# A graph network on one core: node groups moved behind an edge pass, and row weighting moved from VectorE to ScalarE

## The chip, the core and the metric

The kernel runs on one core of one Trainium2 chip. The metric is the device time of one execution in microseconds. The engines have short names in the profile: PE is TensorE (matmuls), PEld its weight loads, DVE is VectorE, ACT is ScalarE, POOL is GpSimd (here it only issues indirect DMAs, which fetch or scatter rows by an index table) and SP is SyncE (it issues plain DMAs). Each engine works through its own list of instructions in order and waits on semaphores that the others raise.

## The reference

A graph with 100,000 nodes of 128 features and 50,000 edges, sorted by destination, goes through four residual layers, each followed by a layer norm (`_layernorm`):

```python
x = _layernorm(x + L0(x))   # three sparse products Z = A Z; concat[x, Z1, Z2, Z3] @ W + b
x = _layernorm(x + L1(x))   # MLP (128 -> 256 -> 128) of x and sum, max, mean of edge attributes
x = _layernorm(x + L2(x))   # attention over the edges: q, k, v, skip; softmax by destination
x = _layernorm(x + L3(x))   # (x + 3 A x) / 4
```

A sparse product A Z fetches row `src` of Z for each edge, multiplies it by the edge's weight, and sums the rows of edges with the same destination:

```python
msgs = edge_vals[:, None] * Z[edge_col]
return jax.ops.segment_sum(msgs, edge_row, num_segments=N_NODES)
```

Only destinations of edges have anything but zero in A x. All other nodes depend on their own row alone.

## The kernel before

Rows are handled in groups of 512 (four tiles of 128). There are 196 node groups, in 49 iterations of four (the four buffer slots), and 98 edge groups, in 25 iterations. The kernel does all nodes as if they had no edges, does the rows that edges touch besides, and scatters the corrected rows over the result at the end. In order of time:

1. Preparation, with a sort of the indices on VectorE, while GpSimd fetches the rows of the destinations.
2. The node stage: `N0` = 11 iterations of node groups alone. A node group is `chain_a` (first product), a norm, `chain_b1` (turn), `chain_b2` (first MLP layer), `chain_c` (second MLP layer, L1125), a norm, `chain_d1` and `chain_d2` (turn, skip product), a norm.
3. The first pass: 25 iterations with a node group and an edge group in each step. The edge group's rows are fetched by GpSimd (`z_gather(0)`), weighted, turned so that edges lie along the free axis, scanned with `tensor_tensor_scan` (a running sum per destination), turned back and stored.
4. The second pass: `N2` = 13 iterations with a node group and two edge groups in each step (`z_gather(1)`). It needs the stored sums of the whole first pass.
5. The source stage: for each edge group the third product (`z_gather(2)`, `z_weigh(2)`, `z_turn(2)`, `z_scan(2)`) and the fetch of the source's own row (`x_gather`, `x_turn`, `x_src`), then the first two layers for these rows; beside it scans over the edge attributes (`attr_scan`).
6. The destination stage, the attention stage, and the last stage: `z_gather(3)`, `z_weigh(3)`, turn, `z_scan(3)`, turn back, `fin_sum`, square, `power` (row sums of squares), `std`, and the final norm, which GpSimd scatters into the output. In the last stage 13 of 25 iterations of results are held in free buffers until the plain copy of the node results, 28 pieces issued by ScalarE (`copy_pieces`), has ended.

In between GpSimd issues small index scatters (`codes`, L788), 392 in all; the counts `VB0`, `VB1`, `VC0`, `VG1` to `VG3` say how many stand where. `VB1` stand ahead of the first pass, `VC0` are spread over its groups, `VG1` stand behind it.

The order of each engine is written out with `steps`. Each stage of a list has a lag: at step g the engine does that stage for group g minus lag, in the order of the list. In the source stage the lists, with lags, are, on TensorE: turn of x1 (2), `chain_a` (1), `chain_b2` (2), turn of x2 (4), `z_turn` (0), `x_turn` (0), `chain_c` (3), skip (4); on VectorE:

```python
steps(dve, EI, (norm2("s"), 4), (z_weigh(2), 0), (power("s", 0), 1), (norm1("s"), 1), (z_scan(2), 0),
      (layer2("s"), 3), (power("s", 1), 3), (attr_scan, 0), (power("s", 2), 4), (attr_mean, 0),
      (norm("s", 2, lambda s: bSK, x3, "ln3_out", x3_free), 4), peeled=1)
```

on ScalarE:

```python
steps(act, EI, (square("s", 0), 1), (std("s", 0), 1), (relu("s"), 2), (seed_mm1("s"), 0), (x2_out("s"), 4),
      (x_src, 0), (square("s", 1), 3), (seed_mlp("s"), 2), (std("s", 1), 3), (x1_out("s"), 1), (square("s", 2), 4),
      (std("s", 2), 4), peeled=1)
```

So at step g VectorE weighs group g, sums the rows of g - 1, scans g, and does layer2 of g - 3. `std` waits for `power` of the same group, `z_turn` for `z_weigh`, `z_scan` for `z_turn`, `layer2` for `chain_c`. A fetch into a slot waits for the turn of the group that was in the slot before. Many operations share a line: L1008 are all turns on TensorE, L1958 all row sums, L1973 all norms, L1989 all weightings, L2008 all scans, L751 all fetches, L764 all scatters of rows. The tiles tell them apart: `gat` holds the fetched rows.

Of the kernel before, what the change touches and what calls it, by code (L numbers as in the profile page):

```python
# [26 lines left out]
P = 128  # L27
T = 4
# [15 lines left out]
def gnn_kernel(nc, x_fm, x_rows, src_g, dst_g, dnext_g, src_flat, dst_flat, w_flat, attr_fm,  # L44
# [14 lines left out]
    N2 = -(-EI // 2)  # L59
    N0 = NI - EI - N2  # L60
    LF = P
# [13 lines left out]
    with ctx:  # L75
# [3 lines left out]
        def dram(name, shape, dt=F32):  # L79
# [12 lines left out]
            "q_out": ("x1T", NI + 2 * EI), "decay": ("relu", NI + 2 * EI), "weight": ("x2T", NI + EI),  # L92
            "att_src": ("z_rows", 2 * EI), "gathered_x": ("gathered_d", 0), "ld_attr": ("st_xd", EI * 16),
        }
# [243 lines left out]
        PAYC = 32  # L338
        VB0, VB1, VC0, VG1, VG2, VG3 = 34, 60, 98, 40, 36, 24
        assert XD0 % SL == 0 and EG - XD0 <= (N0 - 1) * SL and PAYC <= N0 * SL and LF % PAYC == 0  # L340
        assert VB0 + VB1 + VC0 + VG1 + VG2 + VG3 <= EC and LF * 4 <= SL * G
# [13 lines left out]
        def half(stage, e):  # L355

            def one(i, s):
                zi = i * 2 + s // 2
                if not isinstance(i, int) or zi < EI:
                    stage(zi, (2 * s + e) % SL)  # L360
            return one

# [49 lines left out]
        def seq(k, i):  # L412
            return i + k * EI
# [25 lines left out]
        def _(sp):  # L439
# [150 lines left out]
            def pay_store(i, s):  # L590
                k = i * SL + s
                if k < PAYC:
# [7 lines left out]

            steps(sp, EI, (node_load(N0), 0), (x1_store(N0), 3), (zT_store(0), 4), (zE_store(0), 6), (x4_store(N0), 5),
                  (spmm_rows(0), 1), peeled=1)

            steps(sp, N2, (node_load(N0 + EI), 0), (x1_store(N0 + EI), 3), (two(zT_store(1)), 4), (x4_store(N0 + EI), 5),
                  (two(spmm_rows(1)), 2), (two(zE_store(1)), 5), peeled=1)
# [320 lines left out]
        def _(pe):  # L926
# [203 lines left out]
            def chain_d1(kind, i, s):  # L1130
# [5 lines left out]
                if kind == "d":  # L1136
                    prior(pe, "x2sel", s, i)
                else:

                    ahead = (s + 2) // SL  # L1140
                    ends_at = {"node": [N0, N0 + EI, NI], "s": [EI]}[kind]
# [40 lines left out]
            b1, a, b2, d1, c, d2 = node(N0)  # L1182
            steps(pe, EI, b1, a, (z_turn(0), 2), b2, d1, c, (z_back(0), 3), d2, peeled=1)
            all_slots(pe, "x2T", N0 + EI)
            b1, a, b2, d1, c, d2 = node(N0 + EI)
            steps(pe, N2, b1, a, (half(z_turn(1), 0), 2), (half(z_back(1), 0), 3), b2, d1, c, (half(z_turn(1), 1), 2),
# [81 lines left out]
        def _(act):  # L1268
# [139 lines left out]
            def codes_out(i, s):  # L1408
                if void(act, i, s, ("codes_out", i, 1)):
# [6 lines left out]
            steps(act, N0, *node(0))  # L1416
            steps(act, EI, *node(N0)[:6], (z_rows(0), 4), (codes_out, 2), *node(N0)[6:], peeled=1)
            steps(act, N2, *node(N0 + EI)[:6], (half(z_rows(1), 1), 4), *node(N0 + EI)[6:9],
                  (half(z_rows(1), 0), 3), *node(N0 + EI)[9:], peeled=1)
            all_slots(act, "st_z2", 2 * EI * 16)  # L1420

            def x_src(i, s):
                if void(act, i, s, ("x_src", i, 1)):
# [4 lines left out]

            steps(act, EI, (square("s", 0), 1), (std("s", 0), 1), (relu("s"), 2), (seed_mm1("s"), 0), (x2_out("s"), 4),
                  (x_src, 0), (square("s", 1), 3), (seed_mlp("s"), 2), (std("s", 1), 3), (x1_out("s"), 1), (square("s", 2), 4),  # L1430
# [45 lines left out]

            steps(act, EI, (copy_pieces, 0), (square("fin", 3), 2), (std("fin", 3), 2), unrolled=True)


        @block.vector  # L1480
        def _(dve):
# [578 lines left out]
            p0, n1, l2, p1, p2, n2, n3 = node(N0)  # L2060
            steps(dve, EI, p0, (z_scan(0), 2), n1, l2, (z_weigh(0), 1), p1, p2, n2, n3, peeled=1)
            all_slots(dve, "codes_out", EI)
            p0, n1, l2, p1, p2, n2, n3 = node(N0 + EI)
            steps(dve, N2, p0, (half(z_scan(1), 0), 2), n1, l2, (half(z_weigh(1), 0), 1), p1, p2,
# [22 lines left out]
            def attr_mean(i, s):  # L2087
                if void(dve, i, s, ("attr_mean", i, 1)):
# [4 lines left out]

            steps(dve, EI, (norm2("s"), 4), (z_weigh(2), 0), (power("s", 0), 1), (norm1("s"), 1), (z_scan(2), 0),
                  (layer2("s"), 3), (power("s", 1), 3), (attr_scan, 0), (power("s", 2), 4), (attr_mean, 0),
# [147 lines left out]

            def fin_free(i, s):
                if i == HB - 2:
                    at(dve, "st_x3_", s, 2 * EI * 16)
                elif i == HB:
                    at(dve, "scattered2", s, moved(1, 0, s))
                elif i > HB:
                    reuse(dve, "scattered", s, i - HB, 64)  # L2250

            def fin_norm(i, s):
                dst = [h.rearrange("p (t f) -> p t f", t=T) for h in held[i]] if i < HB else x4s
                norm("fin", 3, lambda s: t2[s], dst, "ln4_out", fin_free)(i, s)

            steps(dve, EI, (z_weigh(3), 0), (power("fin", 3), 3), (z_scan(3), 1), (fin_norm, 3), (fin_sum, 2), unrolled=True)


# [51 lines left out]
```

## Time and profile before

| what | value |
|---|---|
| median of 3 runs | 6072.8 us (6069.09 to 6074.92) |
| the profiled execution | 6074.08 us, its span 6072.2 us |
| busy: PE, PEld | 4362.9 us (72%), 3182.1 us (52%) |
| busy: DVE, ACT, POOL | 4394.4 us (72%), 3146.3 us (52%), 4430.8 us (73%) |
| TensorE's mean granted clock | 0.869 of full speed |
| data moved | 1151.65 MB |

Shares of the whole span say little here, since the stages have different limits; the prediction reads each stage by itself. In a timeline a row is one instruction or several alike that follow each other (x4). The bracket tells how long the engine stood idle before it, and what released it; "issue" is time in which nothing that the profile shows was waited for.

### The profile page before, as it was taken

Reading aid. Unit: us, or ns where it says so; the run is one execution under the profiler, and the core shown is the slowest. Engines: PE = TensorE matmul, PEld = TensorE weight load, DVE = VectorE, ACT = ScalarE, POOL = GpSimd, SP = SyncE. Lnnn points to the kernel's source line nnn. Section 1 sums busy time; section 2 is a strip of 40 time slices with the busy share of each in tenths; the row PEclk is TensorE's granted clock in tenths of the full one; section 3 lists DMA queues with packets and bytes.
Section 4 is the critical chain, followed back from the end, with each engine's and each line's share of the span. In section 5 each row is a group of like instructions: output and inputs, shape, how many; then the busy total and the mean of one; then the engine's idle time right before and its main releaser. Section 6 shows DMA issues by size and latency. Waiting matters only on the chain. (4 is left out here: it accounts for less than half of the span.)

```text
span 6072.2 us, 102714 instructions
## 1 busy us (share of the span) xinstructions
PE 4362.9 (72%) x25328; PEld 3182.1 (52%) x25328; DVE 4394.4 (72%) x8168; ACT 3146.3 (52%) x6667; POOL 4430.8 (73%) x4339
## 2 busy tenths in 40 slices
PE   1059899998888799999989999888878873422200
PEld 0047688886666677777765555544444442211100
DVE  8966699997888688888865555599999995743300
ACT  0047688886666455555544444378888881110000
POOL 7777566667777777777757777577777766777777
PEclk9999999999999899999999999988888885555555
DMA  5377488886888799999977777634444438943311
GB/s 126 100 142 181 132 250 253 251 250 197 286 285 286 198 262 264 263 262 264 262 199 224 226 225 227 197 106 116 114 117 114 114 104 265 328 133 94 92 40 40
DMA packets 1005231, 1151.65 MB, mean 190 GB/s; under 512 B 184599, under 2 KB 641235, under 8 KB 1004182
## 3 DMA queue, kind: packets, MB, share of 16 engines
q1 hardware_dynamic: 831958, 834.69, 46.0%
q0 software_dynamic: 137984, 247.24, 16.8%
q10 hardware_dynamic: 35136, 68.16, 3.1%
q14 instruction: 115, 0.94, 0.1%
q8 instruction: 38, 0.62, 0.0%
HBM read 688.22 MB, written 523.68 MB: 200 GB/s over the span
## 5 line engine op out<-in xcount | busy, mean ns | idle before, releaser
L1008 PE MATMUL bank<-ident,gat 128*128 128x128 f32 x2352 | 423.6, 309 | 633.2 <-DVE zT L2008 558.9
L1111 PE MATMUL bank<-x1T,W1x 128*128 128x512 f32 x1568 | 764.9, 600 | 24.5 <-ACT x1T L1304 24.5
L1125 PE MATMUL bank<-W2s,hT 128*128 128x128 f32 x6272 | 777.8, 277 | 1.0 <-ACT hT L1388 1.0
L1125 PEld LDWEIGHTS bank<-W2s,hT 128*128 128x128 f32 x6272 | 734.5, 193 | 16.8 <-ACT hT L1388 1.7
L1008 PEld LDWEIGHTS bank<-ident,gat 128*128 128x128 f32 x2352 | 305.0, 161 | 760.1 <-issue 576.2
L1314 ACT ACTIVATE mbuf<-t 128x512 f32<-128x512 f32 x490 | 309.9, 633 | 581.3 <-DVE t L2042 309.3
L1388 ACT ACTIVATE hT<-bank,b1u 128x512 f32<-128x512 f32 x784 | 502.9, 679 | 183.7 <-PE bank L1111 183.4
L751 POOL DMA_INDIRECT gat<-XD,s_q x392 | 376.8, 961 | 243.1 <-ACT codes_z L1414 109.8
L1008 PE MATMUL bank<-ident,x 128*128 128x128 f32 x3136 | 481.7, 277 | 94.6 <-DVE x L1973 84.6
L751 POOL DMA_INDIRECT gat<-X,d_x x392 | 397.4, 1014 | 205.3 <-issue 205.0
L788 POOL DMA_INDIRECT VQ<-s_v,s_q x392 | 448.7, 1145 | 119.5 <-issue 117.6
L764 POOL DMA_INDIRECT Y<-x,d_out x392 | 403.4, 1029 | 173.2 <-issue 110.9
L1008 PEld LDWEIGHTS bank<-ident,x 128*128 128x128 f32 x3136 | 371.0, 142 | 283.8 <-DVE x L1973 169.3
L751 POOL DMA_INDIRECT gat<-X,s_src x392 | 402.2, 1026 | 153.4 <-issue 153.1
L1989 DVE TENSOR_TENSOR gat<-gat,wts 128x512 f32<-128x512 f32 x294 | 202.8, 690 | 424.8 <-DMA gat<-X,codes_z 372.4
L751 POOL DMA_INDIRECT gat<-Z2E,codes_z x392 | 419.5, 1070 | 119.9 <-issue 119.6
L751 POOL DMA_INDIRECT x<-in_x_rows,s_src x392 | 414.6, 1058 | 119.5 <-issue 119.5
L2008 DVE TENSOR_TENSOR_SCAN zT<-fB,zT,bank 128x512 f32<-128x512 f32 x392 | 498.1, 1271 | 2.4 <-PE bank L1008 2.2
L751 POOL DMA_INDIRECT zin_<-in_x_rows,mixa x392 | 399.6, 1019 | 130.1 <-issue 112.9
L751 POOL DMA_INDIRECT gat<-X,codes_z x392 | 382.3, 975 | 130.1 <-issue 119.0
L751 POOL DMA_INDIRECT gat<-Z1E,codes_z x392 | 379.3, 968 | 119.5 <-issue 104.2
L1111 PEld LDWEIGHTS bank<-x1T,W1x 128*128 128x128 f32 x1568 | 277.5, 192 | 270.9 <-issue 244.5
(369 smaller groups left out, 11316.5 us busy)
## 6 DMA issues: line engine op xcount, KB each, us to landing
X<-x SPq DMA_DIRECT2D x588, 256.0 KB, 2.6
fB<-row_s_same SPq DMA_DIRECT2D x392, 256.0 KB, 5.1
Y<-x SPq DMA_DIRECT2D x294, 256.0 KB, 3.7
xT<-in_x_fm SPq DMA_DIRECT2D x196, 256.0 KB
ffB<-rows_last_notlast SPq DMA_DIRECT2D x98, 512.0 KB
out_rows<-Y ACTq DMA_DIRECT2D x28, 1792.0 KB
Z1T<-zT SPq DMA_DIRECT2D x98, 256.0 KB
Z1E<-zE SPq DMA_DIRECT2D x98, 256.0 KB
```

The lines of the kernel that those rows point to most:

```text
L751: pool.indirect_dma_start(out=tile[:, t, 0:width], out_offset=None, in_=table, in_offset=bass.IndirectOffsetOnAxis(ap=index[t], axis=0)).t ...
L764: pool.indirect_dma_start(out=table, out_offset=bass.IndirectOffsetOnAxis(ap=index[t], axis=0), in_=rows[t], in_offset=None, bounds_check= ...
L788: pool.indirect_dma_start(out=VQ, out_offset=bass.IndirectOffsetOnAxis(ap=s_q[:, c:c + 1], axis=0), in_=s_v[:, c:c + 1], in_offset=None, b ...
L1008: mm = pe.transpose(dst[:, t, :], tiles[t], ident[:, :])
L1111: mm = pe.matmul(bH[h][:, :, :], W1x[:, cols], x1T[s][:, :], start=kind != "d", stop=True)
L1125: mm = pe.matmul(bMLP[:, t, :], hT[h][s][:, t * P:(t + 1) * P], W2s[:, h, :], start=False, stop=h == HC - 1, skip_group_check=True)
L1314: act.activation(sq[k % 3][s % 2], [bT1, t2[s], bSK, t2[s]][k][:, :, :], ACT.Square).then_inc(S(f"squared{k}", s), 1)
L1388: a = act.activation(hT[h][s][:, :], flat(bH[h]), ACT.Relu, bias=b1u[:, h:h + 1])
L1989: dve.tensor_tensor(gat[s][:, :, 0:P], gat[s][:, :, 0:P], weight.to_broadcast([P, T, P]), ALU.mult).then_inc(S("weighted", s), 1)
L2008: dve.tensor_tensor_scan(zT[s][:, :], fB[s][:, :], flat(bIN), zT[s - 1][:, G - 1:G], ALU.mult, ALU.add).then_inc(S("scanned", s), 1)
```

## The change

First, `N1 = EI + 2`: the loop of the first pass becomes 27 iterations, in whose last two only node groups are done, and `N0` falls from 11 to 9. The edge stages in that loop are wrapped in `passing`, which leaves them out from iteration 25 on. 34 index scatters move from ahead of the first pass (`VB1` 60 to 26) into it (`VC0` 98 to 132). Second, the weighting of the source stage and of the last stage goes from VectorE (one `tensor_tensor` of 128x512) to ScalarE (four `activation` with Copy, 128x128 each, the weight as a scale per partition). Third, the last norm's multiplication goes to ScalarE in the same form (`fin_norm`), while VectorE keeps the reciprocal (`fin_scale`). The diff, without the lines that only follow from the new count:

```diff
-    N0 = NI - EI - N2
+    N1 = EI + 2
+    N0 = NI - N1 - N2
...
-        VB0, VB1, VC0, VG1, VG2, VG3 = 34, 60, 98, 40, 36, 24
+        VB0, VB1, VC0, VG1, VG2, VG3 = 34, 26, 132, 40, 36, 24
...
+        def passing(stage):
+
+            def one(i, s):
+                if not isinstance(i, int) or i < EI:
+                    stage(i, s)
+            return one
...
-            steps(pe, EI, b1, a, (z_turn(0), 2), b2, d1, c, (z_back(0), 3), d2, peeled=1)
+            steps(pe, N1, b1, a, (passing(z_turn(0)), 2), b2, d1, c, (passing(z_back(0)), 3), d2, peeled=N1 - EI + 1)
...
+            def z_weigh(k):
+
+                def stage(i, s):
+                    c = seq(k, i)
+                    if void(act, i, s, ("weighted", c, 1)):
+                        return
+                    at(act, "gathered", s, moved(5 if k == 3 else k, i + 1, s))
+                    for t in range(T):
+                        w = bass.ds((i * SL + s) * T + t, 1)
+                        a = act.activation(gat[s][:, t, 0:P], gat[s][:, t, 0:P], ACT.Copy, scale=wts[:, w])
+                    a.then_inc(S("weighted", s), 1)
+                return stage
...
-            steps(act, EI, (square("s", 0), 1), (std("s", 0), 1), (relu("s"), 2), (seed_mm1("s"), 0), (x2_out("s"), 4),
+            steps(act, EI, (square("s", 0), 1), (std("s", 0), 1), (relu("s"), 2), (z_weigh(2), 0), (seed_mm1("s"), 0),
+                  (x2_out("s"), 4),
...
-            steps(act, EI, (copy_pieces, 0), (square("fin", 3), 2), (std("fin", 3), 2), unrolled=True)
...
+            def fin_norm(i, s):
+                if void(act, i, s, ("ln4_out", x4i("fin", i), 1)):
+                    return
+                ready(act, "scaled", s, i)
+                fin_free(i, s)
+                dst = held[i][s].rearrange("p (t f) -> p t f", t=T) if i < HB else x4[s]
+                for t in range(T):
+                    a = act.activation(dst[:, t, :], t2[s][:, t, :], ACT.Copy, scale=lns[3][2][s][:, t:t + 1])
+                a.then_inc(S("ln4_out", s), 1)
+
+            all_slots(act, "agg_turned", EI)
+            steps(act, EI, (copy_pieces, 0), (z_weigh(3), 0), (fin_norm, 3), (square("fin", 3), 2), (std("fin", 3), 2),
+                  unrolled=True)
...
-            steps(dve, EI, (norm2("s"), 4), (z_weigh(2), 0), (power("s", 0), 1), (norm1("s"), 1), (z_scan(2), 0),
+            steps(dve, EI, (norm2("s"), 4), (power("s", 0), 1), (norm1("s"), 1), (z_scan(2), 0),
...
+            def fin_scale(i, s):
+                if void(dve, i, s, ("scaled", i, 1)):
+                    return
+                _, sd, rs, _ = lns[3]
+                ready(dve, "deviation3", s, i)
+                at(dve, "ln4_out", s, x4i("fin", i))
+                dve.reciprocal(rs[s][:, :], sd[s][:, :]).then_inc(S("scaled", s), 1)
+
+            steps(dve, EI, (power("fin", 3), 3), (z_scan(3), 1), (fin_scale, 3), (fin_sum, 2), unrolled=True)
```

## Rows read from the trace of the kernel before

**Rows 1.** Table of two stages (source, attention): busy time, granted clock, DMA.

```profile
2011.00:3145.00 1134.00, 1018.81 (x7411) 853.21 (x7412) 960.32 (x1460) 604.92 (x1265) 860.46 (x808) 0.99 0.92 253
3936.00:5034.00 1098.00, 862.04 (x3234) 499.55 (x3234) 1003.10 (x2454) 902.77 (x1858) 805.36 (x784) 0.81 0.40 112
```

**Rows 2.** Timeline of GpSimd: start, duration, line, tiles; in brackets idle before and releaser.

```profile
723.95 0.96 POOL L751 DMA_INDIRECT gat<-XD,s_q  x1 [34.80 <-PE bank L1008]
...
1406.41 0.97 POOL L751 DMA_INDIRECT gat<-XD,s_q  x1 [1.28 <-ACT codes_z L1414]
...
1465.12 0.99 POOL L751 DMA_INDIRECT gat<-Z1E,codes_z  x1 [0.30 <-issue]
...
1485.79 0.94 POOL L751 DMA_INDIRECT gat<-Z1E,codes_z  x1 [0.30 <-issue]
...
2009.69 0.98 POOL L788 DMA_INDIRECT VQ<-s_v,s_q  x1 [0.31 <-issue]
2010.98 0.99 POOL L751 DMA_INDIRECT gat<-Z2E,codes_z  x1 [0.30 <-issue]
...
3083.15 0.94 POOL L751 DMA_INDIRECT x<-in_x_rows,s_src  x1 [0.30 <-issue]
...
3145.11 0.98 POOL L751 DMA_INDIRECT gat<-X,d_x  x1 [27.29 <-issue]
```

**Rows 3.** Timeline of VectorE in the source stage.

```profile
2019.87 0.69 DVE L1989 TENSOR_TENSOR gat<-gat,wts 128x512 f32<-128x512 f32 x1 [9.57 <-DMA gat<-Z2E,codes_z]
...
3104.98 0.68 DVE L1958 TENSOR_REDUCE ln1vr<-mbuf 128x4 f32<-128x512 f32 x1
...
3108.14 0.66 DVE L2042 SCALAR_TENSOR_TENSOR t<-x,bank 128x512 f32<-128x512 f32 x1
3109.50 0.69 DVE L1958 TENSOR_REDUCE ln2vr<-mbuf 128x4 f32<-128x512 f32 x1 [0.70 <-ACT mbuf L1314]
...
3115.59 0.68 DVE L1989 TENSOR_TENSOR gat<-gat,wts 128x512 f32<-128x512 f32 x1
3116.19 0.68 DVE L1958 TENSOR_REDUCE ln1vr<-mbuf 128x4 f32<-128x512 f32 x1
```

**Rows 4.** Timeline of TensorE, first turn of the second pass.

```profile
1479.24 0.60 PE L1008 MATMUL bank<-ident,gat 128*128 128x128 f32 x4
```

**Rows 5.** Groups of instructions by form, ScalarE: busy us, mean ns.

```profile
L1353 ACT ACTIVATE x<-t,ln3nm,ln3rs 128x128 f32<-128x128 f32 x392 | 160.0, 479 | 1.9 <-DVE ln4nm L2207 1.9
...
L1340 ACT ACTIVATE ln4sd<-lmv,mixb,mixa 128x1 f32<-128x1 f32 x392 | 118.1, 372 | 0.0
...
L1328 ACT ACTIVATE ln2sd<-ln2vr,epsc 128x4 f32<-128x4 f32 x392 | 116.3, 297 | 70.4 <-DVE ln2vr L1958 70.3
```

**Rows 6.** Timeline of ScalarE in the same source round.

```profile
3105.69 0.30 ACT L1328 ACTIVATE ln1sd<-ln1vr,epsc 128x4 f32<-128x4 f32 x1 [2.60 <-DVE ln1vr L1958]
3105.90 1.25 ACT L1388 ACTIVATE hT<-bank,b1u 128x512 f32<-128x512 f32 x2
3107.07 0.59 ACT L1293 COPY bank<-seed_a 128x512 f32<-128x512 f32 x1
```

**Rows 7.** Timeline of TensorE in the same source round.

```profile
3104.51 0.65 PE L1008 MATMUL bank<-ident,x 128*128 128x128 f32 x4 [0.44 <-DVE x L1973]
3105.12 0.66 PE L1008 MATMUL bank<-ident,gat 128*128 128x128 f32 x4
...
3106.05 1.95 PE L1125 MATMUL bank<-W2s,hT 128*128 128x128 f32 x16
```

**Rows 8.** Timeline of TensorE as the source stage drains.

```profile
3144.42 1.12 PE L1008 MATMUL bank<-ident,x 128*128 128x128 f32 x4 [4.65 <-DVE x L1973]
3145.33 3.36 PE L1125 MATMUL bank<-W2s,hT 128*128 128x128 f32 x16
```

**Rows 9.** Timeline of VectorE in the last stage, a round without waits.

```profile
5074.93 0.68 DVE L1989 TENSOR_TENSOR gat<-gat,wts 128x512 f32<-128x512 f32 x1
...
5078.94 0.68 DVE L1989 TENSOR_TENSOR gat<-gat,wts 128x512 f32<-128x512 f32 x1
```

More of the change, by code:

```diff
@@ L92, in gnn_kernel @@
             "q_out": ("x1T", NI + 2 * EI), "decay": ("relu", NI + 2 * EI), "weight": ("x2T", NI + EI),
-            "att_src": ("z_rows", 2 * EI), "gathered_x": ("gathered_d", 0), "ld_attr": ("st_xd", EI * 16),
+            "att_src": ("z_rows", 2 * EI), "scaled": ("scale34", EI), "gathered_x": ("gathered_d", 0), "ld_attr": ("st_xd", EI * 16),
         }
@@ L338, in gnn_kernel @@
         PAYC = 32
-        VB0, VB1, VC0, VG1, VG2, VG3 = 34, 60, 98, 40, 36, 24
-        assert XD0 % SL == 0 and EG - XD0 <= (N0 - 1) * SL and PAYC <= N0 * SL and LF % PAYC == 0
+        VB0, VB1, VC0, VG1, VG2, VG3 = 34, 26, 132, 40, 36, 24
+        assert XD0 % SL == 0 and EG - XD0 <= N0 * SL and PAYC <= N0 * SL and LF % PAYC == 0
         assert VB0 + VB1 + VC0 + VG1 + VG2 + VG3 <= EC and LF * 4 <= SL * G
@@ L599, in _ @@
                   unrolled=True)
-            steps(sp, EI, (node_load(N0), 0), (x1_store(N0), 3), (zT_store(0), 4), (zE_store(0), 6), (x4_store(N0), 5),
-                  (spmm_rows(0), 1), peeled=1)
-            steps(sp, N2, (node_load(N0 + EI), 0), (x1_store(N0 + EI), 3), (two(zT_store(1)), 4), (x4_store(N0 + EI), 5),
+            steps(sp, N1, (node_load(N0), 0), (x1_store(N0), 3), (passing(zT_store(0)), 4), (passing(zE_store(0)), 6),
+                  (x4_store(N0), 5), (passing(spmm_rows(0)), 1), peeled=N1 - EI + 1)
+            steps(sp, N2, (node_load(N0 + N1), 0), (x1_store(N0 + N1), 3), (two(zT_store(1)), 4), (x4_store(N0 + N1), 5),
                   (two(spmm_rows(1)), 2), (two(zE_store(1)), 5), peeled=1)
@@ L1140, in chain_d1 @@
                     ahead = (s + 2) // SL
-                    ends_at = {"node": [N0, N0 + EI, NI], "s": [EI]}[kind]
+                    ends_at = {"node": [N0, N0 + N1, NI], "s": [EI]}[kind]
                     end = next((e for e in ends_at if i < e), 0) if isinstance(i, int) else 0
@@ L1182, in _ @@
             b1, a, b2, d1, c, d2 = node(N0)
-            steps(pe, EI, b1, a, (z_turn(0), 2), b2, d1, c, (z_back(0), 3), d2, peeled=1)
-            all_slots(pe, "x2T", N0 + EI)
-            b1, a, b2, d1, c, d2 = node(N0 + EI)
+            steps(pe, N1, b1, a, (passing(z_turn(0)), 2), b2, d1, c, (passing(z_back(0)), 3), d2, peeled=N1 - EI + 1)
+            all_slots(pe, "x2T", N0 + N1)
+            b1, a, b2, d1, c, d2 = node(N0 + N1)
             steps(pe, N2, b1, a, (half(z_turn(1), 0), 2), (half(z_back(1), 0), 3), b2, d1, c, (half(z_turn(1), 1), 2),
@@ L1416, in _ @@
             steps(act, N0, *node(0))
-            steps(act, EI, *node(N0)[:6], (z_rows(0), 4), (codes_out, 2), *node(N0)[6:], peeled=1)
-            steps(act, N2, *node(N0 + EI)[:6], (half(z_rows(1), 1), 4), *node(N0 + EI)[6:9],
-                  (half(z_rows(1), 0), 3), *node(N0 + EI)[9:], peeled=1)
+            steps(act, N1, *node(N0)[:6], (passing(z_rows(0)), 4), (passing(codes_out), 2), *node(N0)[6:],
+                  peeled=N1 - EI + 1)
+            steps(act, N2, *node(N0 + N1)[:6], (half(z_rows(1), 1), 4), *node(N0 + N1)[6:9],
+                  (half(z_rows(1), 0), 3), *node(N0 + N1)[9:], peeled=1)
             all_slots(act, "st_z2", 2 * EI * 16)
+            def z_weigh(k):
[9 more added lines that the diff above has]
+                return stage
             def x_src(i, s):
@@ L1475, in copy_pieces, with fin_free @@
                     act.dma_start(out_runs[w, :], src_runs[w, :]).then_inc(S("copied"), 16)
-            steps(act, EI, (copy_pieces, 0), (square("fin", 3), 2), (std("fin", 3), 2), unrolled=True)
+            def fin_free(i, s):
+                if i == HB - 2:
+                    at(act, "st_x3_", s, 2 * EI * 16)
+                elif i == HB:
+                    at(act, "scattered2", s, moved(1, 0, s))
+                elif i > HB:
+                    reuse(act, "scattered", s, i - HB, 64)
+            def fin_norm(i, s):
[10 more added lines that the diff above has]
+                  unrolled=True)
         @block.vector
@@ L2060, in _ @@
             p0, n1, l2, p1, p2, n2, n3 = node(N0)
-            steps(dve, EI, p0, (z_scan(0), 2), n1, l2, (z_weigh(0), 1), p1, p2, n2, n3, peeled=1)
+            steps(dve, N1, p0, (passing(z_scan(0)), 2), n1, l2, (passing(z_weigh(0)), 1), p1, p2, n2, n3,
+                  peeled=N1 - EI + 1)
             all_slots(dve, "codes_out", EI)
-            p0, n1, l2, p1, p2, n2, n3 = node(N0 + EI)
+            p0, n1, l2, p1, p2, n2, n3 = node(N0 + N1)
             steps(dve, N2, p0, (half(z_scan(1), 0), 2), n1, l2, (half(z_weigh(1), 0), 1), p1, p2,
@@ L2242, in fin_sum @@
                                          op0=ALU.mult, op1=ALU.add).then_inc(S("fin_sum", s), 1)
[L2244 to L2256, printed above, removed]
+            def fin_scale(i, s):
[6 more added lines that the diff above has]
+            steps(dve, EI, (power("fin", 3), 3), (z_scan(3), 1), (fin_scale, 3), (fin_sum, 2), unrolled=True)
 def kernel(**inputs):
```

## The prediction

> **What bounds the kernel now.** I read the page first, then one table by stage, then the timeline of each engine inside the stages that the change touches. The page's chain of what ended last is of little use here, since it covers only the last tenth and shows GpSimd. The table by stage says more [rows 1]: in the source stage VectorE is busy 960.32 of 1134 us and ScalarE 604.92, so ScalarE looks like the place with room.
>
> GpSimd's timeline shows where each stage begins [rows 2]. It waits 34.80 us for the end of the node stage before group 4 of the first pass; in that pass it waits about 1.28 us a group, at a pace of 7.34 us (723.95 to 1406.41 is 93 groups). It fetches without a gap from 1465.12 to 2010.98, and in the source stage from there to 3083.15, so 1072 us for 98 groups or 10.94 us each. Then it waits 27.29 us until 3145.11. So the source stage does not end with its fetches.
>
> VectorE's timeline of that stage shows the reason [rows 3]. One round (one edge group) lasts 11.21 us, from the first norm's row sums at 3104.98 to the next at 3116.19. The last weighting is at 3115.59, some 30 us after the last fetch. VectorE works through its round with only short waits, so the round is a loop through VectorE's own order, and 97 of them last from 2019.87 to 3115.59.
>
> **The change, part by part. Eight node groups** go from the node stage to behind the first pass. The work is the same and the order within a group is too, so I cost the move itself at nothing: 144 node groups, with their loads and stores on SyncE's queue, stand ahead of the second pass either way. What moves is GpSimd. The first pass begins eight groups of some 7.3 us earlier, so its last fetch does, and the 40 index scatters behind it end near 1407 instead of 1465. The first 16 fetches of the second pass then lie in their four buffers before anyone wants them. The 17th needs the first turn of the second pass, which TensorE does at 1479.24, 0.60 long [rows 4], behind node work that stays where it was. So the 17th fetch starts near 1480.0 instead of 1485.79 [rows 2]: 5.8 us gained, kept to the end of the second pass because GpSimd has no gap from there on. The 34 scatters moved into the first pass cost 1.29 us each (2009.69 to 2010.98) [rows 2]: 34 × 1.29 = 44 us against 93 × 1.28 = 119 us of waits, so nothing. Without that cover they would cost 44 us. Where they came from, they stood before the 34.80 us wait.
>
> **Weighting in the source stage.** VectorE loses one instruction of 0.60 us a round (3115.59 to 3116.19) [rows 3]. ScalarE gains four of 128x128 with one operand per partition, which no row shows. A row with two such operands takes 479 ns at 128 elements and 372 ns at one, so 0.84 ns an element; one with a single operand takes 297 ns at four elements [rows 5]. That gives 297 + 124 × 0.84 = 401 ns. Four of the two-operand kind occupy 160.0/98 = 1.63 us, so each starts 0.09 us before the one ahead ends, and four new ones last 3 × 0.31 + 0.40 = 1.32 us. The bound above is 1.63.
>
> The point is where these four stand: behind std (0) and relu of the same step, and std waits for VectorE's row sums. Follow the round from the row sums at 3104.98:
> - to std on ScalarE at 3105.69, 0.71; to relu 0.21; to what follows relu 1.17 [rows 6];
> - the four weightings there, 1.32;
> - TensorE's turn of gat, the turn of x, and to the second MLP layer (L1125), 3105.12 to 3106.05, 0.93 [rows 7];
> - from there to VectorE's layer2, 3106.05 to 3108.14, 2.09 [rows 3, 7];
> - from layer2 to the next row sums, 3109.50, 1.36, and on to 3116.19, 6.69, less the 0.60 that is gone [rows 3].
>
> Before, the weighting was on VectorE ahead of the row sums, and the turns ran while std and relu did. Now TensorE's turn waits for ScalarE, the L1125 matmuls queue behind it on TensorE, layer2 waits for them on VectorE, and all of VectorE's later work of the round stands behind layer2. Every link is an engine's own order or a semaphore within one round, so they add up: 0.71 + 0.21 + 1.17 + 1.32 + 0.93 + 2.09 + 1.36 + 6.09 = 13.88 us. Over 97 rounds, 97 × (13.88 − 11.21) = 259 us. What else is queued behind the four on ScalarE (the seed, the x2 copy, the x copy) feeds TensorE only after the L1125 matmuls, so it adds nothing. Two-operand weighting would make it 289. Taking the price of the weighting itself for nothing would still leave 12.56 us a round, 131 us.
>
> TensorE now pauses in each round, about 3.2 us between turning x2 (ending 3105.16) and turning gat, where it had no pause before [rows 7]. In this stage's drain it stood idle 4.65 us, and after that one turn took 0.91 us to the next instruction and the 16 matmuls 3.36 us [rows 8]; in the round they take half of 0.93 and 1.95 [rows 7]. The attention stage, where TensorE is busy 79% of the time, has a mean granted clock of 0.81, so part of it at 1.2 GHz; here it would be busy 10.2 of 13.88 us, 73% [rows 1]. At the lower level the two turns cost 2 × 0.91 − 0.93 = 0.89 more and the matmuls 1.41, which makes a round 16.18 us. Both ends stay open: 13.88 if the clock holds, 16.18 if every round is slow. I take two thirds of the difference, since the pause is directly ahead of this very work: 15.41 us, and 97 × (15.41 − 11.21) = 407 us.
>
> **Last stage.** ScalarE gets two sets of four (1.23 us each until the next instruction), a square and std; VectorE keeps a reciprocal. VectorE's round there was 4.01 us without waits [rows 9]. ScalarE's is 1.23 + 1.23 + 0.68 (square to row sums) + 0.71 + 0.21 [rows 6] = 4.06, a little more with the copies that it issues. GpSimd needs 4 × 1.29 = 5.2 us a group for fetches (16 from 1465.12 to 1485.79) [rows 2] and twice that once it scatters too, so both rounds hide behind it: nothing. Uncovered, each us of a longer ScalarE round would cost 52 us up to the first scatter. ScalarE's new wait for the last aggregate's turn stands behind one that it has already, for the attention stage's scatters. The wait for the copies ahead of the first scatter can shift a little either way.
>
> **Sum.** The profiled execution took 6074.1 us (span 6072.2): 6074.1 − 5.8 + 407 = 6475 us, against which the median of the runs is 1.3 us lower, so 6474.
>
> **Rivals.** *VectorE's relief is the gain.* If the four weightings ran while VectorE was at other work, the round would fall by 0.60 to 10.61 us, below GpSimd's 10.94, and the stage would follow the fetches: GpSimd's 27.29 us of waiting behind it go [rows 2], and the time is 6074 − 27 − 6 = 6041. For it speaks VectorE's busy share [rows 1]; against it the order, which lets std and the turn meet only in series. It decides if the turn of gat starts no later after the row sums than now, 0.14 us (3104.98 to 3105.12). The Trainium skill, "Perfetto Trace Analysis", section "Optimizing Scalar/DVE Operations", says the same: where VectorE is saturated, giving some of its operations to ScalarE can make sense. By it the sum is this rival's; the trace agrees on the busy share, and no row shows room in the loop.
>
> *The clock holds at 2.4 GHz.* Then 6074 − 6 + 259 = 6327. For it: a granted clock of 0.99 in this stage [rows 1]. Against it: rows 8 and the attention stage. The Trainium skill, "TensorE: Matmul & The Clock Gate", section "What's actually happening", has the slow clock as the default which activity lifts; by that the round leans to 16.18.
>
> *The early second pass is worth all 58 us.* If the second pass began when its fetches do, 6475 − 52 = 6423. Against it: the turn at 1479.24 follows node work that does not move [rows 4].
>
> *The change does not reach the path*, as the weighting on ScalarE might fit into the 2.60 us in which it waits for row sums [rows 6]. But it is queued behind that wait, not ahead of it. Time: 6068.
>
> **Chances.** A longer source round with a partly slow clock 0.65, with the clock held 0.24, the early second pass on top of either 0.03; relief 0.06; no effect 0.02. A measurement of this kernel can tell about 0.2% from no change, 12 us. Faster 0.06, same 0.02, slower 0.92. The range goes from just under the held clock, 6310, to a slow clock in every round with the dearer weighting, 97 × (16.49 − 11.21) = 512, so 6580.
>
> **What would show it.** In the profile after: a source stage some 400 us longer; VectorE's round near 15 us with two new waits, ahead of the scan for TensorE's turn and ahead of layer2; ScalarE's weightings of 0.40 us behind relu; TensorE idle about 3 us before turning gat, and granted below 0.95 there; GpSimd in that stage waiting for turns. The 17th fetch of the second pass should follow the first turn at once, and the last stage should keep its length. I am wrong if the four instructions stand elsewhere in ScalarE's order than the code says, or if layer2's matmuls are not behind the turn.

## The result and the profile after

The changed kernel takes 6377.8 us (median of four runs, 6375.3 to 6379.6), the kernel before on the same chip 6071.4 us: a ratio of 1.0504 (95% interval 1.0491 to 1.0518). The prediction said 6474 us in a range of 6310 to 6580, slower. Its direction held and its amount was 96 us too high.

The profiled execution took 6379.6 us, against 6074.1 before, so 305.6 us are to be found. GpSimd's timeline again shows where stages begin (the 17th fetch of the second pass, the first of the source stage and its last, and the first of the destination stage, all four in [rows 2]):

```profile
1480.54 0.94 POOL L759 DMA_INDIRECT gat<-Z1E,codes_z  x1 [49.48 <-PE bank L1016]
...
2002.61 0.99 POOL L759 DMA_INDIRECT gat<-Z2E,codes_z  x1 [0.30 <-issue]
...
3399.07 1.39 POOL L759 DMA_INDIRECT x<-in_x_rows,s_src  x1 [0.30 <-issue]
...
3475.44 0.98 POOL L759 DMA_INDIRECT gat<-X,d_x  x1 [42.31 <-issue]
```

The source stage begins 8.4 us earlier than before (2002.61 against 2010.98) and lasts 1472.8 us (to 3475.44) instead of 1134.1: 338.7 more. The destination and attention stages keep their lengths (+1.8 and -1.1 us). From the last stage's first fetch to its last scatter 1007.8 us go by instead of 1033.2: 25.4 us less, and this the prediction had put at nothing. The sum is -8.4 + 338.7 + 0.7 - 25.4 = 305.6.

The table by stage, for the source and the last stage after (columns as in [rows 1]: length, busy time of PE, PEld, DVE, ACT and POOL, granted clock, DMA share, GB/s):

```profile
2003.00:3475.00 1472.00, 1127.29 (x7409) 953.82 (x7410) 920.18 (x1362) 721.27 (x1658) 876.32 (x808) 0.91 0.70 195
...
5366.00:6378.00 1012.00, 193.70 (x784) 152.67 (x784) 249.08 (x392) 317.51 (x980) 759.69 (x784) 0.50 0.47 147
```

and the last stage before, which no row above shows:

```profile
5034.00:6072.00 1038.00, 215.10 (x784) 140.52 (x784) 377.13 (x588) 91.00 (x196) 781.09 (x785) 0.50 0.46 143
```

In the source stage no engine is near its limit: VectorE is busy 920 of 1472 us, with less work than before, and TensorE 1127, at a clock lower by a twelfth (0.91 instead of 0.99). That is the picture of a chain in series. One round shows it, here in VectorE's timeline:

```profile
2908.29 0.68 DVE L2001 TENSOR_REDUCE ln1vr<-mbuf 128x4 f32<-128x512 f32 x1
...
2912.36 1.28 DVE L2051 TENSOR_TENSOR_SCAN zT<-fB,zT,bank 128x512 f32<-128x512 f32 x1 [1.94 <-PE bank L1016]
2916.00 0.69 DVE L2085 SCALAR_TENSOR_TENSOR t<-x,bank 128x512 f32<-128x512 f32 x1 [2.36 <-PE bank L1133]
2917.39 0.69 DVE L2001 TENSOR_REDUCE ln2vr<-mbuf 128x4 f32<-128x512 f32 x1 [0.70 <-ACT mbuf L1322]
...
2923.48 0.68 DVE L2001 TENSOR_REDUCE ln1vr<-mbuf 128x4 f32<-128x512 f32 x1
```

ScalarE's timeline in the same round:

```profile
2909.00 0.30 ACT L1336 ACTIVATE ln1sd<-ln1vr,epsc 128x4 f32<-128x4 f32 x1 [2.11 <-DVE ln1vr L2001]
2909.20 1.25 ACT L1396 ACTIVATE hT<-bank,b1u 128x512 f32<-128x512 f32 x2
2910.34 1.27 ACT L1440 ACTIVATE gat<-gat,wts 128x128 f32<-128x128 f32 x4
2911.51 0.58 ACT L1301 COPY bank<-seed_a 128x512 f32<-128x512 f32 x1
```

TensorE's timeline in the same round:

```profile
2908.43 0.66 PE L1016 MATMUL bank<-ident,x 128*128 128x128 f32 x4 [0.73 <-DVE x L2016]
2911.66 0.66 PE L1016 MATMUL bank<-ident,gat 128*128 128x128 f32 x4 [2.58 <-ACT gat L1440]
...
2912.59 3.28 PE L1133 MATMUL bank<-W2s,hT 128*128 128x128 f32 x16
```

Follow the times across the engines: row sums at 2908.29, std 2909.00, relu 2909.20, weighting 2910.34 to 2911.61, turn of `gat` 2911.66, second MLP layer 2912.59, layer2 at 2916.00, and 7.48 us later the next row sums. The two waits that the prediction named are there, 1.94 us ahead of the scan and 2.36 us ahead of layer2.

This round lasted 15.19 us, as the matmuls of the second layer took 3.28 us. Three rounds in a row (15.20, 15.27 and 13.93 us) in TensorE's timeline, the turn of `gat` and that layer:

```profile
3208.63 0.66 PE L1016 MATMUL bank<-ident,gat 128*128 128x128 f32 x4 [2.58 <-ACT gat L1440]
...
3209.56 3.28 PE L1133 MATMUL bank<-W2s,hT 128*128 128x128 f32 x16
...
3223.82 1.12 PE L1016 MATMUL bank<-ident,gat 128*128 128x128 f32 x4 [2.58 <-ACT gat L1440]
...
3225.58 2.62 PE L1133 MATMUL bank<-W2s,hT 128*128 128x128 f32 x16
...
3239.10 0.66 PE L1016 MATMUL bank<-ident,gat 128*128 128x128 f32 x4 [2.58 <-ACT gat L1440]
...
3240.03 1.95 PE L1133 MATMUL bank<-W2s,hT 128*128 128x128 f32 x16
```

The table by stage, for TensorE alone in these six stretches (length, busy time, granted clock, DMA share, GB/s), shows the clock that goes with them (the DMA columns mean little over stretches this short):

```profile
3208.63:3209.56 0.93, 0.93 (x9) 1.00 1.37 307
3209.56:3212.84 3.28, 3.28 (x18) 0.55 0.84 241
3223.82:3225.58 1.76, 1.76 (x8) 0.50 0.99 292
3225.58:3228.20 2.62, 2.62 (x17) 0.73 1.06 286
3239.10:3240.03 0.93, 0.93 (x9) 1.00 0.97 328
3240.03:3241.98 1.95, 1.95 (x18) 1.00 0.93 249
```

The pause of 2.58 us stands ahead of all three. In one round the turns run at 1.00 of the clock and the layer at 0.55, most of it at 1.2 GHz, and takes 3.28 us instead of 1.95; in the next the turns run at 0.50, the turn of `gat` takes 1.12 instead of 0.66, and the layer 2.62 at 0.73; in the third all is at full speed. The stage goes mostly in this cycle of three; now and then (six times in the stage) four longer rounds stand between two short ones instead of two. Of 97 rounds 30 are under 14.2 us; behind the first three, which fill the pipeline, these have a mean of 13.86 us, and the longer ones 15.29.

### The profile page after: what moved, and what is told of

Read it like the earlier page. It is cut to its first block and busy times, and to the rows that moved or that the text cites. A ratio compares the mean times of both kernels' runs of the same rounds, so it can differ in the third digit from the quotient of the medians.

```text
span 6377.8 us, 103863 instructions
## 1 busy us (share of the span) xinstructions
PE 4448.0 (70%) x25328; PEld 3296.1 (52%) x25328; DVE 4226.2 (66%) x7874; ACT 3487.7 (55%) x7843; POOL 4422.6 (69%) x4339
## 5 line engine op out<-in xcount | busy, mean ns | idle before, releaser
L1016 PE MATMUL bank<-ident,gat 128*128 128x128 f32 x2352 | 443.3, 320 | 899.5 <-ACT gat L1440 804.3
L1133 PE MATMUL bank<-W2s,hT 128*128 128x128 f32 x6272 | 846.9, 293 | 1.0 <-ACT hT L1396 1.0
L1133 PEld LDWEIGHTS bank<-W2s,hT 128*128 128x128 f32 x6272 | 803.6, 208 | 16.7 <-ACT hT L1396 1.7
L759 POOL DMA_INDIRECT gat<-Z2E,codes_z x392 | 393.7, 1004 | 427.3 <-PE bank L1016 322.9
L1016 PE MATMUL bank<-ident,x 128*128 128x128 f32 x3136 | 498.3, 284 | 99.3 <-DVE x L2016 98.8
L759 POOL DMA_INDIRECT x<-in_x_rows,s_src x392 | 457.7, 1168 | 119.5 <-issue 119.2
L1016 PEld LDWEIGHTS bank<-ident,x 128*128 128x128 f32 x3136 | 385.9, 146 | 287.0 <-DVE x L2016 183.6
L1440 ACT ACTIVATE gat<-gat,wts 128x128 f32<-128x128 f32 x784 | 248.8, 391 | 352.6 <-DMA gat<-X,codes_z 334.1
```

Source lines behind the costliest of these rows:

```text
L759: pool.indirect_dma_start(out=tile[:, t, 0:width], out_offset=None, in_=table, in_offset=bass.IndirectOffsetOnAxis(ap=index[t], axis=0)).t ...
L1016: mm = pe.transpose(dst[:, t, :], tiles[t], ident[:, :])
L1133: mm = pe.matmul(bMLP[:, t, :], hT[h][s][:, t * P:(t + 1) * P], W2s[:, h, :], start=False, stop=h == HC - 1, skip_group_check=True)
L1440: a = act.activation(gat[s][:, t, 0:P], gat[s][:, t, 0:P], ACT.Copy, scale=wts[:, w])
```

## The experiments

**The three parts alone.** The kernel before, with only the node groups' move (`N1 = EI + 2` and the counts of index scatters):

> Only the move of the node groups (with the index scatters). If its whole worth is the earlier 17th fetch of the second pass and what follows from it, GpSimd starts that fetch near 1480.5 us, the source stage begins 8.4 us earlier than before as it did with the whole change (2002.6 against 2011.0), every later stage keeps its length, and the time is 6071.4 - 8.4 = 6063 us, a ratio of 0.9986. If the gain was given back in the source stage, where VectorE sets the pace, the ratio is 1.000; if the fetches were the bound of the second pass from its first group on, it is 6071 - 54 = 6017 us.

Measured: 6069.2 against 6075.0 us, a ratio of 0.9990 (0.9981 to 0.9999); the source stage begins at 2001.98. The 17th fetch of the second pass comes at once behind TensorE's first turn there, as predicted, and GpSimd idles 52 us ahead of it:

```profile
1478.39 0.94 POOL L759 DMA_INDIRECT gat<-Z1E,codes_z  x1 [52.12 <-PE bank L1016]
```

So of the 58 us that the eight groups take, some 6 arrive. The two other outcomes fall: the interval ends just short of 1.000, but the source stage lasts 1134.2 us there, so it gives nothing back. The 8.4 us by which the source stage began earlier in the profiled pair hold some scatter: in the traces of the seven kernels without the move it begins at 2006.6 to 2011.0 us, in those of the seven with it at 1999.4 to 2005.1, and the means lie 6.4 us apart.

Only the last stage's part (weighting and final norm on ScalarE, reciprocal on VectorE):

> Only the last stage's weighting and final norm on ScalarE. Theory: VectorE's two multiplications of 128x512 with both operands in SBUF stretch GpSimd's issuing of fetches and scatters that run at the same moment (1.48 to 1.51 us instead of 0.98); without them GpSimd's busy time in this stage falls from 781 to about 760 us and the stage from 1038 to 1012 us: 6071.4 - 25 = 6046 us, ratio 0.9958. Rival, the one of the prediction: GpSimd covers both rounds, so nothing, 6071 us; then the 25 us in the changed kernel came from the state in which the longer source stage left things.

Measured: 6043.5 against 6075.0 us, ratio 0.9951 (0.9938 to 0.9965). The part is a gain of some 30 us by itself, with GpSimd busy 760 us in the stage; the prediction's "nothing" is wrong.

Only the source stage's part:

> Only the source stage's weighting on ScalarE, at the place where the change has it. If the parts add up, the source stage lasts about 1473 us instead of 1134 and the time is 6071.4 + 338 = 6410 us, ratio 1.056. If the node groups' move had a part in the slower stage, less: below 1.05.

Measured: 6414.5 us, ratio 1.0564 (1.0548 to 1.0580), the stage 1466.3 us. The whole loss is here, and the parts add up: -6 - 31.5 + 339.5 = +302, measured +306.

**Place or engine?** The kernel before, with VectorE's own weighting two places later, behind the row sums and the first norm:

```diff
-            steps(dve, EI, (norm2("s"), 4), (z_weigh(2), 0), (power("s", 0), 1), (norm1("s"), 1), (z_scan(2), 0),
+            steps(dve, EI, (norm2("s"), 4), (power("s", 0), 1), (norm1("s"), 1), (z_weigh(2), 0), (z_scan(2), 0),
```

> The kernel before with one move: VectorE's own weighting in the source stage stands behind the first norm instead of ahead of the row sums. The engine, the instruction and the work are those of before. Theory of the place: the weighting is now behind the row sums, std and the first norm, and the turns, the second MLP layer and layer2 behind the weighting: 1.04 to the reciprocal, 0.24, 0.60, 0.60, about 0.1, then 0.93 + 2.09 + 1.36 + 6.09 = 13.05 us a round instead of 11.21, so 97 x 1.84 = 178 us, 6250 us, and up to 6340 where the slower clock takes part of the rounds. Rival, the price of ScalarE's four instructions is the cost: then this kernel is as fast as before, 6071 us.

Measured: 6369.6 against 6075.0 us, ratio 1.0486 (1.0470 to 1.0502), nearly as slow as the change, without one instruction on another engine. The time lies above the expected 6250 to 6340. Of 97 rounds 40 last under 13.5 us, most of these 13.2 to 13.3, where the sum said 13.05; the slower clock (0.90 in the stage) takes the rest up to 15.8. A round in VectorE's timeline shows the new waits, ahead of the scan and ahead of layer2:

```profile
2905.48 0.68 DVE L1958 TENSOR_REDUCE ln1vr<-mbuf 128x4 f32<-128x512 f32 x1
...
2907.45 0.68 DVE L1989 TENSOR_TENSOR gat<-gat,wts 128x512 f32<-128x512 f32 x1
2908.94 1.28 DVE L2008 TENSOR_TENSOR_SCAN zT<-fB,zT,bank 128x512 f32<-128x512 f32 x1 [0.81 <-issue]
2912.74 0.69 DVE L2042 SCALAR_TENSOR_TENSOR t<-x,bank 128x512 f32<-128x512 f32 x1 [2.52 <-PE bank L1125]
```

The same question from the other side: the changed kernel, with ScalarE's four weightings first in their step:

```diff
-            steps(act, EI, (square("s", 0), 1), (std("s", 0), 1), (relu("s"), 2), (z_weigh(2), 0), (seed_mm1("s"), 0),
+            steps(act, EI, (z_weigh(2), 0), (square("s", 0), 1), (std("s", 0), 1), (relu("s"), 2), (seed_mm1("s"), 0),
```

> The changed kernel with one move: in the source stage ScalarE's four weightings stand first in its step, ahead of the square, std and relu, instead of behind relu. Instructions and engine are those of the change. Theory of the place: the weighting then waits for nothing but the fetched rows, the series is gone and VectorE's relief counts: VectorE's round falls to about 10.6 us, under GpSimd's pace, the stage follows the fetches, some 27 to 60 us shorter than before, and the time is 6071 - 8 - 25 - 27 = 6011 us, down to 5980. Rival, ScalarE's weighting is dear wherever it stands: the round stays near 14.8 us and the time near 6378 us.

Measured: 6019.4 against 6076.8 us, ratio 0.9906 (0.9890 to 0.9921). With the same instructions on the same engine the change as a whole costs 306 us when they stand behind relu, and gains 57 when they stand first. The weightings now run in the time in which ScalarE waited for row sums, as its timeline shows:

```profile
2610.91 1.27 ACT L1440 ACTIVATE gat<-gat,wts 128x128 f32<-128x128 f32 x4
2612.09 0.57 ACT L1322 ACTIVATE mbuf<-bank 128x512 f32<-128x512 f32 x1
```

VectorE behind them comes to its scan without a wait, and to layer2, 3.49 us behind the row sums, with one of 0.25 us:

```profile
2612.88 0.68 DVE L2001 TENSOR_REDUCE ln1vr<-mbuf 128x4 f32<-128x512 f32 x1
...
2614.86 1.27 DVE L2051 TENSOR_TENSOR_SCAN zT<-fB,zT,bank 128x512 f32<-128x512 f32 x1
...
2616.37 0.69 DVE L2085 SCALAR_TENSOR_TENSOR t<-x,bank 128x512 f32<-128x512 f32 x1 [0.25 <-PE bank L1133]
```

A round lasts 11.07 us, the stage 1112.1 us, 22 less than before. That is less relief than expected (10.6 us a round): GpSimd still waits 26.67 us behind its fetches, so the stage does not follow them yet. TensorE's timeline shows what holds the second layer back, a wait for the second norm ahead of the turn of x2, behind which the turn of `gat` stands:

```profile
2613.02 0.65 PE L1016 MATMUL bank<-ident,x 128*128 128x128 f32 x4 [0.73 <-DVE x L2016]
2613.51 0.60 PE L1016 MATMUL bank<-ident,gat 128*128 128x128 f32 x4
```

**What stands behind the weighting.** The changed kernel, with TensorE's second MLP layer ahead of the two turns:

```diff
-                  (of("s", chain_d1), 4), (z_turn(2), 0), (x_turn, 0), (of("s", chain_c), 3), (of("s", chain_d2), 4), peeled=1)
+                  (of("s", chain_d1), 4), (of("s", chain_c), 3), (z_turn(2), 0), (x_turn, 0), (of("s", chain_d2), 4), peeled=1)
```

> The changed kernel with one move: in the source stage TensorE's second MLP layer stands ahead of the turns of the weighted rows and of the sources' rows. ScalarE's order stays. Theory of the series: layer2 then waits only for VectorE's scan (TensorE's wait for the weighting, the turns and the 1.95 us of the layer fall out of the loop, the scan stays in it), so VectorE goes on 1.2 us behind the scan's start, some 2.4 us a round earlier than now: rounds of 11.5 to 12.5 us, a stage of 1150 to 1240 us, 6380 - 97 x 2.6 = 6130 us, 6070 to 6170. Rival, TensorE's order does not matter because VectorE waits for the weighted rows in the scan anyway: 6378 us.

Measured: 6186.5 against 6076.8 us, ratio 1.0181 (1.0165 to 1.0198), 191 us less than the changed kernel, with rounds of 12.81 us and a granted clock of 0.99. The layer's place behind the turns is thus a large part of the loss, and the rival falls; the expected rounds of up to 12.5 us were a little short. In VectorE's timeline layer2 starts 5.34 us behind the row sums, directly behind the scan, then 1.36 and 6.10 to the next: the scan is still behind the weighting, in series.

```profile
2918.48 0.68 DVE L2001 TENSOR_REDUCE ln1vr<-mbuf 128x4 f32<-128x512 f32 x1
...
2922.62 1.28 DVE L2051 TENSOR_TENSOR_SCAN zT<-fB,zT,bank 128x512 f32<-128x512 f32 x1 [2.09 <-PE bank L1016]
2923.82 0.66 DVE L2085 SCALAR_TENSOR_TENSOR t<-x,bank 128x512 f32<-128x512 f32 x1
2925.18 0.69 DVE L2001 TENSOR_REDUCE ln2vr<-mbuf 128x4 f32<-128x512 f32 x1 [0.70 <-ACT mbuf L1322]
```

**The clock.** The changed kernel, with 20 turns of the identity matrix put into TensorE's pause:

```diff
-                        ready(pe, "weighted", s, seq(min(k, 3), i))
                         prior(pe, "scanned", s, seq(min(k, 3), i))
+                        if k == 2:
+                            for _ in range(5):
+                                turn(bIN, [ident[:, :]] * T)
+                        ready(pe, "weighted", s, seq(min(k, 3), i))
```

> The changed kernel with 20 more turns of the identity matrix on TensorE in each round of the source stage, into the bank that the next turn overwrites, at the place where TensorE waits for ScalarE's weighting (2.58 us). They leave the results as they are. Theory of the clock: rounds of 15.2 us are those in which TensorE's turns or its second MLP layer ran at the lower clock after the pause; with the pause filled all rounds last 13.9 us, the stage's granted clock goes from 0.91 to 0.98 or more, and the time falls by 94 x 1.0 = 90 us to about 6285. Rival, the longer rounds have another cause (transfers, GpSimd): no change, 6378 us, or longer if the added turns outlast the pause.

Measured: 6283.8 against 6076.8 us, ratio 1.0342 (1.0325 to 1.0358), 94 us less than the changed kernel by doing more. From the fourth on, all rounds last 13.77 to 13.93 us, and in the table by stage the source stage's granted clock is 0.99:

```profile
2004.00:3378.00 1374.00, 1232.07 (x9351) 1062.47 (x9352) 920.38 (x1363) 721.14 (x1658) 884.26 (x809) 0.99 0.76 209
```

So the price of 338.7 us can be split by the lengths of the stage. With the pause filled it lasts 1373.6 us: 239 more than before, which is the series (13.86 us a round instead of 11.30, the mean of the 97 before), and 99 less than in the changed kernel, which is the clock's share. The 191 us of the run before this one, whose clock was 0.99 too, hold that share as well: its rounds are 1.05 us shorter than 13.86, some 102 us in all, and this is what the layer's place behind the turns costs in the series itself.

**Without the source stage's part.**

> The changed kernel with the source stage's weighting back on VectorE at its old place: the node groups' move and the last stage's part alone. If the parts add up: 0.9990 x 0.9951 = 0.9941, so 6036 to 6040 us beside a kernel before at 6071 to 6075. If the two gains share a cause, only the larger of them: 0.995.

Measured: 6042.7 against 6076.8 us, ratio 0.9945 (0.9931 to 0.9959). It lies between the two expected outcomes, and its interval holds the sum (0.9941) and the last stage's part alone; this run does not tell them apart.

**The best version.** The kernel with the weightings first, and TensorE's two turns ahead of the turn of x2:

```diff
-                  (of("s", chain_d1), 4), (z_turn(2), 0), (x_turn, 0), (of("s", chain_c), 3), (of("s", chain_d2), 4), peeled=1)
+                  (z_turn(2), 0), (x_turn, 0), (of("s", chain_d1), 4), (of("s", chain_c), 3), (of("s", chain_d2), 4), peeled=1)
```

> The kernel with the weightings first in ScalarE's step, and one more move: in the source stage TensorE turns the weighted rows and the sources' rows ahead of the turn of x2, for which it waits 0.73 us a round for VectorE's second norm. In the run without this move VectorE waits 0.25 us a round for the second MLP layer, which stands behind all three turns, and a round lasts 11.07 us; GpSimd's fetches need 10.73 us a group. Theory: the two turns fill TensorE's wait, the layer starts 0.7 us earlier, VectorE's wait goes, and the round falls to 10.7 to 10.8 us: 98 x 0.3 = 30 us less, 5990 us beside a kernel before at 6073, ratio 0.986. Rival: the round is already at GpSimd's pace; then 6019 us, ratio 0.991.

Measured: 5989.2 against 6080.1 us, ratio 0.9856 (0.9841 to 0.9871), faster than both kernels. A round lasts 10.78 us, the stage 1084.7, and VectorE comes to layer2 without a wait:

```profile
2607.69 1.27 DVE L2051 TENSOR_TENSOR_SCAN zT<-fB,zT,bank 128x512 f32<-128x512 f32 x1
2608.87 0.66 DVE L2085 SCALAR_TENSOR_TENSOR t<-x,bank 128x512 f32<-128x512 f32 x1
```

**The last stage: what lengthens GpSimd's issues?** GpSimd's timeline in the kernel before:

```profile
5499.75 1.02 POOL L764 DMA_INDIRECT out_rows<-x,s_out  x1 [0.30 <-issue]
5501.07 1.48 POOL L764 DMA_INDIRECT out_rows<-x,s_out  x1 [0.31 <-issue]
5502.86 0.98 POOL L764 DMA_INDIRECT out_rows<-x,s_out  x1 [0.30 <-issue]
```

VectorE's at the same moment:

```profile
5500.99 0.69 DVE L1989 TENSOR_TENSOR gat<-gat,wts 128x512 f32<-128x512 f32 x1 [6.20 <-DMA gat<-X,codes_z]
5501.60 0.68 DVE L1958 TENSOR_REDUCE ln4vr<-mbuf 128x4 f32<-128x512 f32 x1
```

The scatter issued while VectorE multiplies takes 0.5 us more. In the last stage before, 36 of 784 issues take over 1.2 us by the timeline's two decimals; in the changed kernel none does. What decides is which of the two began first. All 51 issues over 1.1 us in that stage began 0.04 to 0.42 us behind the start of such a multiplication (the weighting or the final one), and end 0.81 to 0.89 us behind its end; the 125 that began ahead of one and ran into it took 1.00 us at most. The length of VectorE's instruction is not the cause: beside row sums (0.68 us) or scans (1.27 us) alone no issue took over 0.99 us.

The kernel before, with both multiplications left on VectorE, but with one operand of rows each:

```diff
+                    if kind == "fin":
+                        for t in range(T):
+                            a = dve.tensor_scalar(dst[s][:, t, :], src(s)[:, t, :], rs[s][:, t:t + 1], None, ALU.mult)
...
+                    if k == 3:
+                        for t in range(T):
+                            a = dve.tensor_scalar(gat[s][:, t, 0:P], gat[s][:, t, 0:P], wts[:, bass.ds(g + t, 1)], None, ALU.mult)
...
```

> The kernel before; in the last stage VectorE keeps the weighting and the final multiplication, but as four instructions of 128x128 with the factor as one operand per partition, instead of one of 128x512 with two operands of rows. If it is the two operands of rows in SBUF that stretch GpSimd's issues, GpSimd's busy time in the stage falls from 781 to about 760 us and the time to 6045 us, ratio 0.9955, as with ScalarE doing the work. If any work of VectorE's on SBUF tiles stretches them, GpSimd stays at 780 us or more and the time at 6071 us.

Measured: 6057.2 against 6080.1 us, ratio 0.9962 (0.9948 to 0.9976). No issue takes over 1.2 us, and GpSimd is busy 763.5 us in the stage, with VectorE still doing the work: the form was the cause of that part. The scatters of `x` show it, in the kernel before and in this one (shortest, median and longest, in ns):

```profile
L764 POOL DMA_INDIRECT out_rows<-x,s_out x232: 977/986/1519, 5342.8 to 6047.2; - x116
...
L764 POOL DMA_INDIRECT out_rows<-x,s_out x232: 977/982/1059, 5336.4 to 6030.4; - x116
```

The time did not reach ScalarE's 0.9951 in its median; a wait of 6.8 us at the sixth group of fetches (the next run's expectation calls it the ninth) is still there.

The other sign, the final multiplication done twice:

> The kernel before; in the last stage VectorE does the final multiplication of 128x512 twice over (the same result both times), 98 instructions more. If these instructions stretch GpSimd's issues, by some 0.11 us for each of the 196 that are there now, GpSimd's busy time in the stage rises from 781 to 790 us or more and the time by 10 to 14 us, ratio 1.002. If GpSimd's pace does not depend on them, no change: VectorE is busy 377 of 1038 us there and has room.

Measured: 6086.5 against 6080.1 us, ratio 1.0009 (1.0000 to 1.0018), 57 issues over 1.2 us, GpSimd busy 789 us. The sign is as expected and the amount smaller (6 us, not 10 to 14); but kernels whose last stage is that of before show 36 to 58 such issues and 781 to 791 us, so this run proves little.

The one-operand form, with VectorE's scan of the group before ahead of the next weighting:

> The kernel before with the last stage's two multiplications on VectorE as four instructions with one operand of rows, as in the run on their form, and with VectorE's scan of the group before ahead of the weighting of the next one. In the run on the form GpSimd's busy time fell as with ScalarE (762.8 us), but a wait of 6.8 us at the ninth group of fetches stayed, which ScalarE's version does not have: there VectorE's first scan stands behind its second weighting, which waits for rows. Theory: with the scan ahead, that wait goes and the time is that of ScalarE's version, ratio 0.995. Rival: the rest of ScalarE's gain is the relief of VectorE; then the ratio stays at 0.996, as in the run on the form.

Measured: 6054.8 against 6079.2 us, ratio 0.9960 (0.9947 to 0.9974): a miss for the theory, and the rival's number, whose reason the run does not show. The wait shrank only to 5.2 us, and GpSimd waited 7.7 us for the copies in front of its first scatter instead (6.4 in the run on the form). What gives ScalarE's version its last 10 us ahead of the first scatter stays open. A difference that the traces show is that its copies start with three pieces instead of four before the first rows arrive; this was not tried.

## Why the prediction was right, and where not

**Source stage: the mechanism held, the clock term was mis-sized.** The sum for a held clock was 13.88 us a round; the rounds in which the clock held measure 13.86, and with TensorE's pause filled all do from the fourth on. Link by link, in the round shown above: std after 0.71 (0.71 foreseen), relu 0.20 (0.21), the weightings 1.14 later (1.17) and 1.27 long (1.32), turns to second layer 0.93 (0.93), and in a round with the clock held 13.86 in all. The estimate of 401 ns for the weighting that no row showed came to 391. TensorE paused 2.58 us, where 3.2 were foreseen: without VectorE's weighting between the second norm and the row sums, the turn of x2 starts 0.14 us behind the row sums, no longer 0.47 ahead.

The step that was off is "I take two thirds of the difference". The dear round of 16.18 us charged the turns and the layer's whole length at the lower level. One round of 97 reached it (16.27, the fifth, with turns and layer wholly at 0.50): otherwise the low level lies over the layer's greater part in one round, over the turns and part of the layer in the next, over neither in the third. The 97 rounds lasted 14.78 us in the mean instead of 15.41, which makes 97 × 0.63 = 61 us. The round before that was followed, 11.21, was 0.09 below the mean of its stage, which makes 9 more. So the stage grew by 338.7 us where 407 were forecast; with the last stage's 25 us and the second pass's 3, below, this makes the 96 us, to within 1. All three errors point the same way, so none of them hid another. The filled pause confirms the term by itself: 94 us in the times, 99 in the length of the stage, instead of 97 × 1.53 = 148.

**Last stage: the step "both rounds hide behind it: nothing" failed.** It took GpSimd's own pace as fixed. ScalarE's round was indeed hidden, but GpSimd's pace depended on what VectorE does beside it. The term is -25 us in the profiled pair, of which 20.7 are GpSimd's shorter busy time (780.8 to 760.1 us over its 784 issues). The 1.48 us scatter could have been read in the trace of before. The Trainium skill states the rule, in "SBUF — State Buffer", section "SBUF: two separate sides": VectorE and GpSimd share a pair of ports, which a VectorE instruction with two SBUF inputs holds against a GpSimd instruction that reads SBUF, if it started first. The trace agrees: the long issues (1.48 us against 0.98) all began during a two-operand multiplication, none that began ahead of one is long, and none took over 1.2 us with one operand.

**Node groups: right.** 5.8 us were predicted; the 17th fetch came 5.3 us earlier, the source stage 8.4 in this pair of traces, and the part alone gave 6.

**Rivals.** VectorE's relief, given 0.06, was wrong for this change but right for the kernel: it needs the weighting ahead of what ScalarE waits for. In the reordered run the turn of `gat` no longer waits for the weighting. It starts 0.63 us behind the row sums (2612.88 to 2613.51), not within the 0.14 that the rival asked for, and the round is 11.07 us and not 10.61; with TensorE's turns moved too it is 10.78. The held clock (6327 us) was missed by 51 us, nearer than the forecast. The early second pass did not come: GpSimd's 49.48 us in front of the 17th fetch are what it would have been worth.

## What to carry to other kernels

Before work goes to an engine with idle time, find what that engine waits for at the place where the work will stand, and follow the round through the engines: here the same four instructions made a stage 339 us longer behind one wait and 22 us shorter in front of it. Price a pause on TensorE separately from the chain that makes it, by the rows at both levels, and ask over which part of the work the low level will lie: here it was a part only. And look whether an engine that sets the pace has instructions of uneven length; what stands beside the long ones may be the cheaper thing to change.

## What the runs showed of the hardware

- GpSimd's issue of an indirect DMA took up to 1.52 us instead of 0.98 when it began during a VectorE multiplication of 128x512 with both operands in SBUF (51 issues over 1.1 us in the last stage before, each ending 0.81 to 0.89 us behind the multiplication). It took 1.00 us at most when it began ahead of one (125 issues), and never over 1.2 us beside four multiplications of 128x128 with one operand of rows.
- Adding 20 turns a round to TensorE in a pause of 2.6 us made the kernel 94 us faster: the granted clock of the stage went from 0.91 to 0.99.
- The lower level came mostly in a cycle of three rounds, two with a stretch at it and one without, though the pause of 2.58 us stood in every round.
